# Unused bf16 matmuls on the identity in TensorE's long waits and before each narrow tile's weighted sum

## The reference

```python
x = x + _L0_xattn_ref(_layernorm(x), ctx, ctx, ...)   # 16 heads of 16
x = x + _L0_ffn_ref(_layernorm(x), ...)               # one fp8 product
x = x + _L1_xattn_ref(_layernorm(x), ctx, ...)        # 16 heads of 64
x = x + _L1_ffn_ref(_layernorm(x), ...)               # 8 experts, top 2
x = x + _L2_xattn_ref(_layernorm(x), ctx, ...)        # transformer block
x = x + _L2_ffn_ref(_layernorm(x), ...)               # 8 experts choose tokens
x = x + _L3_xattn_ref(_layernorm(x), ctx, ctx, ...)   # 16 heads of 16, mask
x = x + _L3_ffn_ref(_layernorm(x), ...)               # int8 fake quantisation
```

## Time and profile before

| | |
|---|---|
| median of 3 executions | 1663.53 us (1661.6 to 1664.51) |
| the profiled execution's own time | 1666.42 us |
| its span, first to last instruction | 1664.6 us |
| mean granted TensorE clock over the span | 0.932 |
| TensorE matmul / weight load busy | 86% / 72% |
| VectorE, ScalarE, GpSimd busy | 67%, 46%, 38% |

### The profile page before, as it was taken

One profiled execution on the slowest core, in us unless ns is written; L12 is line 12 of the kernel. 1 busy time (PEld: TensorE's weight loads), 2 busy tenths in 40 slices (PEclk: granted clock), 3 DMA queues, 4 the chain that ended last, 5 costly groups with the idle time before them and its releaser, 6 DMA issues. The chain is left out here.

```text
span 1664.6 us, 25770 instructions
## 1 busy us (share of the span) xinstructions
PE 1423.5 (86%) x9598; PEld 1202.9 (72%) x9598; DVE 1111.8 (67%) x2381; ACT 766.8 (46%) x1321; POOL 636.5 (38%) x437
## 2 busy tenths in 40 slices
PE   6997679997859999996889997669999999699874
PEld 4886568896559999995677766247888889568622
DVE  7786868886646767673464553676666665567587
ACT  2555645542146767672454333113334343245565
POOL 1560236565025555551132223023665555245100
PEclk9997989998979999998899998889999999899787
DMA  5000000000546777755000000422444453400001
GB/s 191 1 2 5 1 1 1 1 1 1 191 153 199 223 217 222 217 138 143 1 1 1 1 1 0 141 100 83 95 99 95 89 110 51 99 1 2 1 1 51
DMA packets 94177, 122.04 MB, mean 73 GB/s; under 512 B 12300, under 2 KB 79271, under 8 KB 94055
## 3 DMA queue, kind: packets, MB, share of 16 engines
q1 hardware_dynamic: 72935, 91.56, 17.1%
q0 software_dynamic: 21120, 28.85, 9.5%
HBM read 94.95 MB, written 25.43 MB: 72 GB/s over the span
## 5 line engine op out<-in xcount | busy, mean ns | idle before, releaser
L2756 POOL DMA_INDIRECT ch_total<-ch_y,ch_index x64 | 107.4, 1678 | 118.8 <-DVE ch_y L2971 101.1
L1335 POOL DMA_INDIRECT t_total<-t_y,t_index x46 | 98.5, 2142 | 131.1 <-DVE t_y L1456 116.4
L3828 POOL TENSOR_TENSOR L_s<-L_s,L_mx 128x1232 f32<-128x1232 f32 x32 | 76.5, 2391 | 117.3 <-DVE L_mx L3920 117.3
L2886 ACT ACTIVATE ch_silu<-ch_ps 128x512 f32<-128x512 f32 (+1 forms) x68 | 39.0, 573 | 175.7 <-PE ch_ps L842 175.7
L840 PE MATMUL ch_ps<-ch_hT_hi,ch_w_hi 128*128 128x512 f32 (+1 forms) x272 | 106.1, 390 | 10.7 <-DVE ch_hid L2961 7.3
L840 PE MATMUL t_ps<-t_hT_hi,t_w_hi 128*128 128x256 f32 x368 | 106.7, 290 | 6.0 <-DVE t_w_lo L1443 6.0
L840 PE MATMUL t_ps<-t_w_hi,t_act_hi 128*128 128x256 f32 x368 | 105.8, 288 | 0.0
L841 PE MATMUL t_ps<-t_hT_lo,t_w_hi 128*128 128x256 f32 x368 | 105.7, 287 | 0.0
L842 PE MATMUL t_ps<-t_hT_hi,t_w_lo 128*128 128x256 f32 x368 | 105.6, 287 | 0.0
L841 PE MATMUL ch_ps<-ch_hT_lo,ch_w_hi 128*128 128x512 f32 (+1 forms) x272 | 105.1, 386 | 0.0
L842 PE MATMUL ch_ps<-ch_hT_hi,ch_w_lo 128*128 128x512 f32 (+1 forms) x272 | 105.0, 386 | 0.0
(11 more groups left out here) (596 smaller groups left out, 4531.3 us busy)
## 6 DMA issues: line engine op xcount, KB each, us to landing
t_w_in<-in_L_ffn_w1T SPq DMA_DIRECT2D x23, 1024.0 KB, 4.9
t_w_in<-in_L_ffn_w2T SPq DMA_DIRECT2D x23, 1024.0 KB, 5.7
ch_w_in<-in_L_ffn_w SPq DMA_DIRECT2D x24, 512.0 KB, 4.0
x<-in_x SPq DMA_DIRECT2D x4, 512.0 KB, 4.9
t_total<-x SPq DMA_DIRECT2D x1, 2048.0 KB
t_rows<-t2d_h SPq DMA_DIRECT2D x1, 2048.0 KB
x<-t_total SPq DMA_DIRECT2D x8, 256.0 KB, 4.4
tb_w<-in_L_xattn_w SPq DMA_DIRECT2D x2, 1024.0 KB, 10.1
```

Source lines behind the costliest of these rows:

```text
L1335: nc.gpsimd.indirect_dma_start(out=total, out_offset=bass.IndirectOffsetOnAxis(ap=index[:, 2 * j + u:2 * j + u + 1], axis=0), in_=y[:, j % ...
L2756: nc.gpsimd.indirect_dma_start(out=total, out_offset=at(s, u), in_=y[:, s % 2, u, :], in_offset=None, compute_op=ALU.add).then_inc(added[s ...
L3828: nc.gpsimd.tensor_tensor(s[:, n % G], s[:, n % G], spread(mx[:, n % G, :], 2, [P, H, KEYS]), ALU.subtract).then_inc(shifted, 1)
```

## The change

Seven places get unused bf16 matmuls. Six are calls of `keep_busy` with 256 columns each: 64 before `queries(2, 0)` in wide attention; 44 before `layer1(1)` in the top-2 experts; in the transformer block 14 in iterations 0 and 1 after `turn_first`, 6 and 8 more in iteration 1, and 30 in iteration 9; 70 in the int8 feed-forward before the second product, with a wait on `hh_ready` in front, since they write the PSUM bank that the first product used. The seventh is in narrow attention: 4 of 128 columns for each tile from the second on, between `turn_output` and `attend`.

```diff
             turn_rows(6)
+            keep_busy(nc, ps[:, 7, 0:2 * P], k.ident[:].bitcast(BF16), 64)
             queries(2, 0)
...
             for j in range(TILES):
+                if j == 1:
+                    keep_busy(nc, ps[:, 7, 0:2 * P], k.ident[:].bitcast(BF16), 44)
                 layer1(j)
...
                     scores(a)
+                if it == UNITS + 1:
+                    keep_busy(nc, ps[:, 0, 0:2 * P], filler, 30)
                 if 0 <= f:
                     turn_rows("y2", f, n2, rows_ready[2])
...
                     feed_in(f)
+                if it <= 1:
+                    keep_busy(nc, ps[:, 7, 0:2 * P], filler, 14)
                 if 0 <= c < UNITS:
                     turn_rows("y1", c, n1, rows_ready[1])
                 if a < UNITS:
                     turn_probs(a, 0)
+                if it == 1:
+                    keep_busy(nc, ps[:, 7, 0:2 * P], filler, 6)
                 if 0 <= c < UNITS:
                     context_scores(c)
...
                     feed_out(f)
+                if it == 1:
+                    keep_busy(nc, ps[:, 7, 0:2 * P], filler, 8)
                 if 0 <= c < UNITS:
                     turn_context(c)
...
             pe.wait_ge(row_taken, 1)
+            pe.wait_ge(hh_ready, NG * IC - 1)
+            keep_busy(nc, ps[:, 0, 0:2 * P], k.ident[:].bitcast(BF16), 70)
             for n in range(2 * NG):
...
                 if n:
                     turn_output(n - 1)
+                    keep_busy(nc, ps[:, 6, H * HEAD:H * HEAD + P], k.ident[:].bitcast(BF16)[:, 0:P], 4)
                 attend(n)
```

## The result

| | before | after |
|---|---|---|
| median | 1664.02 us (1661.6 to 1666.69, 4 runs) | 1653.02 us (1649.64 to 1654.28, 4 runs) |
| ratio of the times | | 0.9921, 95% interval 0.9895 to 0.9948 |
| the profiled execution: own time, span | 1666.42, 1664.6 us | 1654.28, 1652.5 us |
| mean granted clock | 0.932 | 0.943 |

The account below looks back on a forecast made before the run. The granted clock, mean 0.932, falls after TensorE's waits and behind narrow attention's thin weighted sums. Six terms sum to 13.6 us: 1666.42 gives 1652.8, less half the profile-to-median difference 1651.5 us, range 1645 to 1660.

Parts of the forecast that it names:

- Narrow attention, 6.1 us: Both narrow stages: four free fillers before each weighted sum hold the clock, four long tiles become normal; bounds -6.6 to 8.0.
- The rival that the narrow tiles keep their falls: Narrow attention: 0.22 us of fillers in 5.8 us is too little, leaving 7.5 us of gain; 1658.9 or 1656, chance 0.27.
- the delayed weighted sum: Narrow attention: fillers outlast the free 0.41 us, each of 30 tiles late by up to 0.4 us; 1669, chance 0.05.
- Wide attention, 2.0 us: 64 fillers in the 8.56 us wait: the next 24 queries take 2.85 instead of 4.86 us; bounds 0 to 2.1.
- all of it passes on: Wide attention: turned probabilities behind the queries are ready since 238.6, so the full 2.0 us gain carries through.
- the rival that the gain is taken up elsewhere: VectorE or GpSimd become the bound behind each filled place; 1663 us, chance 0.06.
- Top-2 experts, 1.8 us: 44 fillers in the 5.98 us wait: 18 distances take 2.2 instead of 3.98 us, gain kept; bounds 0 to 1.9.
- Transformer block, start, 1.8 us: Fillers in the first waits: context scores gain 0.87 us and the context's weighted sum 0.91; bounds 0 to 3.4.
- if the clock then stays up: Transformer block start: condition for context scores at 1.09 instead of 1.96 us and their weighted sum at 1.13 instead of 2.04.
- Transformer block, end, 1.0 us: 30 fillers before `feed_in`, 2.8 us possible at full clock, but a fall judged likely in idle time left; bounds 0 to 3.0.
- Int8, 0.9 us: 70 fillers before the second product: first 24 matmuls 2.8 instead of 5.3 us, saving VectorE's idle 0.94; bounds 0 to 1.8.
- the cap of 16.6 us: Whole kernel: limit on any gain, estimated from the skill's ramp penalty of under 1%; the upper bounds together come to 20 us.

Follow-up runs that it names:

- moved: Changed kernel with the four fillers of each narrow tile in front of the first turn of probabilities, not the weighted sum: 1663.90 us, ratio 1.0.
- the experiment: Changed kernel without the 64 fillers in wide attention and the 44 in the top-2 experts: 1651.12 us, ratio 0.9911.

## Why the prediction was right, and where it wasn't

The sum of the terms was 13.6 us against the profiled execution's 1666.42; the profiled execution after took 12.1 us less. The forecast of 1651.5 lies between the two medians of the changed kernel, 1653.02 and 1649.47. So the total was right. Of its six terms one was right (top-2 experts), one failed (wide attention), one of the right size came by another path (the transformer block's start), one isn't shown (its end), and two of the right mechanism came out smaller (narrow attention, int8).

**Narrow attention, 6.1 us: the mechanism was right, and a hole in it was missed.** The reason given, that the clock falls behind the thinnest stretch and that dense work there holds it, is what the runs bear out best. I took the distances of all weighted sums in the 11 profiles that have fillers (or transposes) in this place: of the 312 distances from a filled tile to the next, none is long. The three profiles without them there (before, without narrow fillers, moved) have 11 long ones among 84, tile 0 not counted. The price of nothing was right too. What was overlooked is that tile 0 has none. In the nine profiles where it is left bare, 9 of 18 first tiles are long, by 1.3 to 3.2 us, in the three without any fillers in this place 1 of 6, and in the two where it is filled none of 4. That fits a fall that comes where no filler is, but numbers as small as these don't show it. In the profile after, the second stage's stretch is 6.0 us shorter: 4.5 by the three long tiles, and 2.2 behind the last weighted sum (11.0 to 8.8), mostly by the two projections that I had only in the upper bound, less 0.6 in front of the first one. The first stage's is 1.5 longer: 3.2 for tile 0, less 1.6 for the long tile that went, and 1.4 more in front of the first weighted sum, less 1.4 behind the last. So the total of 4.5 instead of 6.1 is partly made of other parts than the sum's. The rival that the narrow tiles keep their falls is out for the tiles that have fillers, and so is the delayed weighted sum: the distance between tiles went from 5.81 to 5.80 us.

**Wide attention, 2.0 us: the term failed at "all of it passes on".** The queries gained 2.6 us, and from the stage's start to the experts it is 0.3 (263.6 to 263.3). I had looked at what stands right behind the queries and not at the end of the stage, where waits of 1.1 to 2.3 us lie among the last tiles and the clock falls at several of them, nor at the fillers at half the clock behind. It is the rival that the gain is taken up elsewhere, for this stage alone, and by TensorE's own clock instead of by another engine.

**Top-2 experts, 1.8 us: right.** 18 distances 2.23 us as forecast, the stage 2.2 shorter, 2.6 by the experiment. It is kept because no wait comes in the 240 us behind.

**Transformer block, start, 1.8 us: near in size, wrong place.** The context's scores stayed at 1.96 and its sum at 2.04 us, the clock having fallen at 788 all the same. The 1.5 us came from what I had called a side branch: `attend_self` 1.56 us instead of 2.12, and the scores of iteration 0 1.47 instead of 2.63. Timeline of TensorE, before and after:

```profile
782.12 2.12 PE L1955 MATMUL tb_ps<-tb_y,tb_pT 128*128 128x256 f32 x6 [0.46 <-ACT tb_pT L2097]
784.03 2.63 PE L1934 MATMUL tb_ps<-tb_y0T 128*128 128x128 f32 x8
```

```profile
779.71 1.56 PE L1958 MATMUL tb_ps<-tb_y,tb_pT 128*128 128x256 f32 x6 [0.46 <-ACT tb_pT L2108]
781.11 1.47 PE L1937 MATMUL tb_ps<-tb_y0T 128*128 128x128 f32 x8
```

The step that failed is "if the clock then stays up", and behind it "in a wait of about the same length". The wait was 2.55 us before; but TensorE came to it sooner while ScalarE's normed rows didn't come as much sooner, so it had grown to 3.7 us (783.02 to 786.69). 14 fillers left 2.14 us of it, and I had argued from the 2.53 us one row above that this is too long, but only for the end of the block.

**Transformer block, end, 1.0 us: 1.5 by the two profiles, near 0 by the experiments.** The clock fell as before, at 1017.3 in the wait of 1.17 us, and how much of `feed_in` it took differs from kernel to kernel with the fillers and without. The lower bound of the term was the better value, as the reason given for it (the wait left is too long) says by itself. It is also where the rule of the Trainium skill on transposes (TensorE: Matmul & The Clock Gate, Part 4) put it, but for that the idle time is reason enough. With both waits filled it is 7.17 us, a gain of 2.8.

**Int8, 0.9 us: first step right, then given back in part, 0.6.** The first pair of parts ran in 2.79 us after a wait of 2.55, VectorE's 0.94 us went. The new wait wasn't met at once, it took 0.43 us, which cost nothing; and 10.98 - 7.6 leaves 3.4 us, not 2.9 as the prediction has it. I had not asked where the clock would fall next: it fell in the second and the last pair, where waits of 2.44 and 2.09 us are left.

**What filled the sum up** were differences that no filler stands next to. The middle of the transformer block is 1.4 us shorter after, by one fall less (905), and the choice experts 1.0 us longer; the same stretches vary by as much and more from one profile to the next (choice experts: 274.8 to 281.2 us in the 14 profiles). Part of the agreement in the total is therefore luck.

**Median against profile.** I took off half the difference between the profiled execution and the median. The kernel before reads 1664 us in all four series, so its first three runs weren't low, and the forecast should have been made against 1664: 1650.4.

By the Trainium skill (TensorE: Matmul & The Clock Gate, Part 1) the ramp penalty is under 1% of a typical kernel's span. It says that of the slow matmuls at a kernel's start; the cap of 16.6 us on every later fall too was my reading. The change and the forecast stay under it. With more of the waits filled the kernel gained 26.3 us, 1.6%, and its clock is still only 0.960; the measurement decides, and that cap would have misled.

## What to carry to other kernels

Where the granted clock falls behind thin work or a wait, and the engine waits there anyway, matmuls that nobody reads can buy it back for nothing, as in the narrow tiles and the second tile of the top-2 experts; price them by the distance of their starts, put them into the wait directly in front of the thin work, and not somewhere else in the tile. Fill every such place of a stage, down to its end, and leave little idle (in the transformer block 0.39 us held where 2.14 did not): in wide attention and the int8 stage a fall prevented in one place came at a later bare one. Measure the wait again with the fillers in place, since a faster stretch in front makes it longer. Before counting a gain at a stage's start, follow it to the stage's end.

## What the runs showed that I had not expected

- Idle time before a fall doesn't have one length: a wait of 2.14 us brought one (transformer block), one of 2.55 us did not (int8), and behind the thin weighted sums 0.24 us is enough.
- Two fp32 transposes of the identity per tile hold the clock as four bf16 matmuls do (1651.39 and 1649.47 us, intervals of the ratios 0.9901 to 0.9951 and 0.9895 to 0.9945).
- Executions of one kernel differ by 3.4 us (6 runs, transposes) to 15 us (23 runs of the kernel before), and which weighted sum the clock falls behind differs between kernels that are the same up to it.
- A stretch that no edit touches, the choice experts, differs by 6.4 us between profiles. That is more than most terms of the sum, so a difference of two medians of 6 runs doesn't say which stretch it comes from; the checkpoints do.
- Fillers that run at half the clock take twice as long and hold up what stands behind them: 11 of 512 columns took 4.90 us instead of 2.54.
